# Held-back projection pieces, masks woven into two products, and rotating PSUM banks in a graph-attention kernel

## The reference, cut to what matters

```python
# x: 1250 x 768; src, dst: 41250 edges (20000 random ones in both directions, and loops)
def _L0_gnn_ref(x, edge_index, W, b):
    src, dst = edges plus one loop for each node
    deg = segment_sum(1, dst); dis = rsqrt(deg)
    return segment_sum((x @ W)[src] * (dis[src] * dis[dst]), dst) + b

def gat_conv(x, edge_index, W, a_src, a_dst, bias, heads, out_ch, concat):
    xl = (x @ W).reshape(n, heads, out_ch)
    e = leaky_relu((xl * a_src).sum(-1)[src] + (xl * a_dst).sum(-1)[dst], 0.2)
    e = exp(e - segment_max(e, dst)[dst])
    alpha = e / (segment_sum(e, dst)[dst] + 1e-16)
    out = segment_sum(xl[src] * alpha, dst)
    return (heads side by side, or their mean) + bias

def _L1_gnn_ref(x, ...):
    h1 = relu(layer_norm(gat_conv(x, W1, ..., heads 4, 256 each))) + (x @ Wr1 + br1)
    return layer_norm(gat_conv(h1, W2, ..., 1 head of 768)) + (h1 @ Wr2 + br2)

x = _layernorm(x + _L0_gnn_ref(x, edges, W0, b0))
x = _layernorm(x + _L1_gnn_ref(x, edges, ...))
```

## Time and profile before

| | |
|---|---|
| median of 3 runs | 905.65 us (905.5 to 906.43) |
| the profiled execution | 904.68 us, of it 902.9 us from its first instruction to its last (the span) |
| mean granted clock of PE | 0.968 of full speed |
| busy | PE 836.2 us, VectorE 679.6 us, ScalarE 256.1 us, GpSimd 60.4 us |
| counting, to the last degrees | about 21 to 156 us |
| first aggregation | 161 to 229 us |
| masks | 230 to 246 us |
| projection `xl`, residual product | 246 to 413 us |
| first attention | 415 to 621 us |
| second layer | 621 to 903 us |

### The profile page before, as it was taken

How to read it: one execution, slowest core, us unless ns; L and a number is a source line. 1 busy time by engine, 2 the same in 40 slices (tenths; PEclk the granted TensorE clock), 3 DMA queues, 4 the chain that set the end, 5 groups by cost and what they waited for, 6 DMA issues and landing times.

```text
span 902.9 us, 13798 instructions
## 1 busy us (share of the span) xinstructions
PE 836.2 (93%) x5086; PEld 546.4 (61%) x5086; DVE 679.6 (75%) x1180; ACT 256.1 (28%) x451; POOL 60.4 (7%) x82
## 2 busy tenths in 40 slices
PE   2999999899699999999999988968999999999995
PEld 2577776466555444446888867856656666655553
DVE  5988885778656668797777789783985579955686
ACT  3344443500012010114444354341213118730000
POOL 2000001000202000100000000000210000000021
PEclk8799999899899999999999989989999999999998
DMA  8000000314221213513210113210222732322231
GB/s 289 2 1 2 2 2 22 139 46 163 95 110 47 70 34 120 192 66 136 90 50 30 29 48 105 63 37 1 70 70 71 245 111 71 105 71 70 70 105 67
DMA packets 23373, 70.42 MB, mean 78 GB/s; under 512 B 2628, under 2 KB 3548, under 8 KB 23182
## 3 DMA queue, kind: packets, MB, share of 16 engines
q1 hardware_dynamic: 21438, 61.80, 19.6%
q0 software_dynamic: 1872, 7.78, 2.7%
HBM read 49.26 MB, written 20.31 MB: 77 GB/s over the span
## 4 chain that ended last, share of the span: by engine, by line
PE 72%; DVE 12%; issue 11%; POOL 2%; ACT 1%; DMA 1%; DVEq 0%; SPq 0%; POOLq 0%; ACTq 0%
PE psum L636 24%; PE psum L817 14%; PE psum L788 13%; PE psum L879 11%; PE psum L665 4%; DVE arena L1323 2%; DVE arena L1338 2%; DVE arena L1354 1%; DVE arena L1186 1%; PE psum L670 1%; DVE arena L1362 1%; POOL arena L570 1%; DVE arena L1228 1%; PE psum L661 1%; PE psum L838 1%
## 5 line engine op out<-in xcount | busy, mean ns | idle before, releaser
L636 PE MATMUL psum<-arena 128*128 128x512 f16 (+1 forms) x1080 | 228.9, 364 | 0.9 <-DVE arena L1213 0.9
L817 PE MATMUL psum<-arena 128*128 128x257 f32 x800 | 181.6, 389 | 22.2 <-ACT arena L953 20.9
L886 ACT ACTIVATE arena<-psum 128x160 uint16<-128x160 f32 (+6 forms) x226 | 94.9, 465 | 332.7 <-PE psum L636 79.5
L817 PEld LDWEIGHTS psum<-arena 128*128 128x128 f32 x800 | 154.7, 195 | 47.8 <-issue 16.6
L636 PEld LDWEIGHTS psum<-arena 128*128 128x128 f16 x1080 | 100.4, 98 | 104.1 <-issue 5.3
L788 PE MATMUL psum<-arena 128*128 128x512 f16 x960 | 159.2, 328 | 2.4 <-ACT arena L953 2.4
L788 PEld LDWEIGHTS psum<-arena 128*128 128x128 f16 x960 | 94.4, 98 | 65.0 <-ACT arena L953 2.8
L879 PE MATMUL psum<-arena 128*128 128x512 f16 (+2 forms) x600 | 98.4, 326 | 0.0
L961 ACT ACTIVATE arena<-arena 128x640 f32<-128x640 f32 x80 | 66.0, 829 | 87.4 <-DVE arena L1323 87.4
L1228 DVE CUSTOM_DVE_ANT_0 arena<-psum,arena 128x256 bf16<-128x256 f32 (+1 forms) x100 | 46.7, 527 | 52.5 <-PE psum L636 33.1
L1218 DVE CUSTOM_DVE_ANT_0 arena<-arena 128x1280 bf16<-128x1280 bf16 x50 | 71.0, 1487 | 16.7 <-DMA arena<-as_scratch 12.9
(11 more groups left out here) (162 smaller groups left out, 618.4 us busy)
## 6 DMA issues: line engine op xcount, KB each, us to landing
arena<-in_L_gnn_W_dram SPq DMA_DIRECT2D x14, 384.0 KB, 5.9
r_scratch<-arena SPq DMA_DIRECT2D x10, 512.0 KB, 2.6
arena<-uv_scratch SPq DMA_DIRECT2D x16, 320.0 KB, 3.9
arena<-r_scratch SPq DMA_DIRECT2D x10, 512.0 KB, 3.6
x_scratch<-arena SPq DMA_DIRECT2D x10, 384.0 KB, 4.6
arena<-x_scratch SPq DMA_DIRECT2D x10, 384.0 KB, 3.5
r_scratch<-arena SPq DMA_DIRECT2D x10, 384.0 KB, 2.6
arena<-r_scratch SPq DMA_DIRECT2D x10, 384.0 KB, 4.0
```

What stands on the lines that cost most here:

```text
L636: ins = pe.matmul(o[:, a:b], part[:, k, ds(t * P, P)], w[:, k, a:b], start=(not begun and k == 0 and n == 0 and m == 0), stop=(k == kn - 1 ...
L817: last = pe.matmul(p_att[:, j, 0:HID + 1], pf[n % PSLOTS][:, j * P:(j + 1) * P], xl[ch % H][:, k, 0:HID + 1], start=(k == 0), stop=(k == T ...
L886: act.activation(out_, in_, ACT.Copy, scale=scale).then_inc(signal, 1)
```

## The change

Three things, in one diff.

1. **Held pieces.** The last five pieces of the projection of tile 9 (`HELD`) are taken out of the counting loop and stand behind the last degrees, ahead of the flag's matmul. The other pieces are spread over the same 80 blocks, 49 where 54 were, so that a tile takes about nine blocks. The transposes of tile t + 2 stand in the block after the one in which tile t ends (`FETCH`: blocks 8, 17, 26, 35, 44, 53, 61 and 70), VectorE's part of them five blocks later, and ScalarE reads a finished tile in the block in which it ends. ScalarE reads tile 9 between the third and the fourth `hs_hi`.
2. **Masks woven in.** The first product starts behind the first two transposes, and the ten mask transposes, with the transposes of tiles 2 and 3, stand between the six parts of the first product and the six of the second. `x1t_low(0)` stands on VectorE ahead of the normalising of tile 9. The masks' slots move to banks 6, 7 and 0, 1. The copy of the first product stands behind the last mask on VectorE.
3. **Banks in rotation.** Chunk 0 uses banks 0 to 4, chunk 1 banks 5, 6, 7, 0, 1, and so on over eight banks; the second four chunks go over six banks. Each chunk's first matmul into a bank waits for that bank's last reader. `sums` takes one instruction for each run of neighbouring banks: two in chunks 1, 3, 4, 5 and 6.

```diff
+HELD = 5
+FETCH_LAG = 5
+HS_FIRST = 3
 def pieces_until(b):
-    return max(0, min(b + 1 - W_LAG, KD)) if b < SUBS else KD + (b + 1 - SUBS) * (T - 1) * KD // (NB - SUBS)
+    return max(0, min(b + 1 - W_LAG, KD)) if b < SUBS else KD + (b + 1 - SUBS) * ((T - 1) * KD - HELD) // (NB - SUBS)
+def done_block(t):
+    return next(b for b in range(NB) if pieces_until(b) >= (t + 1) * KD)
+FETCH = {done_block(t) + 1: t + 2 for t in range(T - 2)}
+ATT_BANKS = [[(ch * C1 + j) % 8 for j in range(C1)] for ch in range(H)]
+ATT_BANKS += [[(4 + ch * C1 + j) % 6 for j in range(C1)] for ch in range(H)]
...
-        X1_ORDER = [s for i in range(T) for s in [("tr", t) for t in (2 * i, 2 * i + 1) if t < T] + [("xl", i)]]
+        X1_ORDER = [("tr", 0), ("tr", 1)]
+        X1_ORDER += [s for k in range(KD) for s in [("part", 0, k)] + ([("neg", k - 3)] if k >= 3 else [])] + [("xl", 0)]
+        X1_ORDER += [s for k in range(KD) for s in [("part", 1, k)] + [[("neg", 3)], [("tr", 2)], [("neg", 4), ("tr", 3)], [("neg", 5), ("neg", 6)], [("neg", 7)], [("neg", 8), ("neg", 9)]][k]] + [("xl", 1)]
+        X1_ORDER += [s for i in range(2, T) for s in [("tr", t) for t in (2 * i, 2 * i + 1) if t < T] + [("xl", i)]]
...
 (PE, counting)
-                if j == 0 and 1 <= t < T - 1:
-                    transposes(t + 1)
+                if b in FETCH:
+                    transposes(FETCH[b])
...
             for t in range(T - TAIL, T):
                 degrees(t)
+            for q in range(T * KD - HELD, T * KD):
+                project_nodes(q // KD, q % KD)
             pe.wait_ge(S["over_ok"], 1)
...
 (PE, attention)
-                    if k == 0 and ch:
-                        pe.wait_ge(S["att_read"], (ch - 1) * C1 + j + 1)
+                    if k == 0 and bank_reader(ch, j):
+                        pe.wait_ge(S["att_read"], bank_reader(ch, j))
...
 (ScalarE)
             for t in range(T):
+                if t == HS_FIRST:
+                    node_evict(T - 1)
+                    act.wait_ge(S["h_read"], T)
                 act.activation(hs_hi[:, t, :], ...
...
 (VectorE)
                 dve.tensor_tensor(y, y, par_rows[:, 2, 0:D], ALU.add).then_inc(S["dve"], 1)
+                if t == T - 1:
+                    x1t_low(0)
...
-                dve.tensor_scalar(ssum, p_att[:, :, HID:HID + 1]..., SOFTMAX_EPS, None, ALU.add)
+                for a, b in bank_runs(ch):
+                    first = ATT_BANKS[ch][a]
+                    dve.tensor_scalar(ssum[:, a:b], p_att[:, first:first + b - a, HID:HID + 1]..., SOFTMAX_EPS, None, ALU.add)
```

135 lines of the change are left out of this document (80 added, 55 removed).

## The result

| | before | after |
|---|---|---|
| median | 905.88 us (4 runs, 905.5 to 906.43) | 894.88 us (4 runs, 893.02 to 895.81) |
| the profiled execution | 904.68 us, span 902.9 | 893.02 us, span 891.1 |
| mean granted clock of PE | 0.968 | 0.980 |

The changed kernel takes 0.9875 of the time (95% interval 0.9858 to 0.9893): 11.0 us won, where 8.1 were forecast. In a second set of runs, beside the experiments, it was 895.14 against 905.33, 0.9882 (0.9864 to 0.9901), 10.2 us. 897.5 was forecast, with a range from 892.5 to 901.0. The direction was right, and the size 2 to 3 us too small. One execution of one experiment, the transposes one block later, took 4842.58 us and is left out of its median and ratio.

The account below looks back on a forecast made before the run. The chain of waits was taken as the bound, PE holding most of it. Held pieces 0.5 + masks 3.8 + banks 3.8 = 8.1 us won, 905.65 − 8.1 = 897.5 us for the median; range 892.5 to 901.0.

Parts of the forecast that it names:

- All three terms: Counting loop and behind it: five pieces removed win 4.95 us; seven transpose waits cost 3.1, the late flag 1.3.
- The four small waits: Woven masks: PE waits 0.75 us ahead of mask transposes 4 and 5, then 0.35 and 0.6 at the end.
- the half fall of the clock: Woven masks: a clock fall behind PE's new wait would cost 1.85 us; half was counted, 0.9.
- The first number of the sum: Woven masks: PE waits 2.0 us for `x1t_low(0)` before the first product, in 2.0 + 24.7 + 2.45 = 29.2 us.
- The gain per start: Attention, starts of chunks 1 to 3: PE's wait for ScalarE's eviction goes, 1.08 us each, 3.24 in all.
- the second sum: Attention: a second `sums` instruction on VectorE where a chunk's banks are split, costing 0.19 us.
- VectorE is the bound there: Second four attention chunks: VectorE mostly bounds, so waits ahead of chunks 5 to 7 stay; 0.25 us won each time.
- the matmul done ahead: Attention chunks 5 to 7: one matmul of five goes early into a free bank, 0.44 less 0.19 us each time.
- Covered transposes: Rival, counting loop: transposes of x never wait, held pieces give 3.6 us, 11.2 in all, 894.4 us; chance 0.15.
- Rotation that doesn't free the chunks: Rival, attention: the wait returns at the fourth matmul, rotation gives 0.5 of 3.8 us, 900.8 us; chance 0.13.
- The woven stretch at 1.2 GHz: Rival, masks and first products: PE's clock stays low, 14.8 us lost there, 10.5 slower in all, 916 us; chance 0.03.

Follow-up runs that it names:

- the two experiments: Each against the changed kernel: transposes of x one block later, 892.37 us; the flag's matmul behind the first held piece instead of the fifth, 893.67 us.
- the early sums: Changed kernel with chunk 6's sums 3.6 us earlier on VectorE and its eviction one step earlier, 889.04 us; with chunks 4 and 5 earlier too, 888.19 us.
- the same group: Changed kernel run again beside the held pieces undone (0.9887), masks put back (0.9934) and banks fixed (0.9948); ratios to the kernel before; changed kernel 895.14 us, 0.9882.
- the rotated traces: Seven traces with banks in rotation: two of the changed kernel, five of variants; 115.46 to 118.23 us from the sums of chunk 3 to the first product behind the attention.
- the changed kernel's second trace: Trace of the changed kernel run once more, nothing altered; median 895.14 us, ratio 0.9882 to the kernel before; the trace's span 894.2 us.
- the last three with early sums: Changed kernel with sums of chunks 4 to 6 earlier, 888.19 us; plus later transposes and earlier flag, 882.82; plus two W2 row blocks a step later, 877.89.
- the second trace of before: Trace of the kernel before run once more, nothing altered; 906.59 us.

## Why the prediction was right, and where it was too small

*Held pieces (0.5 forecast, 0.3 shown).* All three terms stood. Seven new waits came at the seven places, at 0.43 us each against 0.44 (the kernel with the transposes a block later). The loop became shorter by 2.87 − 0.93 = 1.94 us in the first pair of traces, and by 1.74 against the kernel without held pieces; 1.85 was worked out. `hs_lo` came 1.34 to 1.41 us late behind the degrees (1.5 forecast), and the flag was the cause. That the part is worth almost nothing followed from the sum, and the two experiments show that 3.5 and 0.9 us more were to be had in it.

*Masks (3.8 forecast, 5.3 in the stretch).* The walk through the order was close: 24.7 us of work, and 3.94 us of waits against 2.0 + 2.45. The four small waits were 2.00 instead of 2.45. The term that was mis-sized is the half fall of the clock: behind 1.94 us PE stayed at 1.00 in all ten traces with this wait, so 0.9 us too much was given back. Some chance of it was there: behind the 2.44 us from which it was read the clock fell in ten of the fourteen traces, and ahead of the attention it fell once behind 2.25 us. Its price was off as well: where the fall does come, it costs 2.93 us, since it lies over the products and lasted 6.0 us, and not the 1.85 that the transposes had shown. The first number of the sum, the 2.0 us wait, decided the sign: with 5.61 us in its place the same weaving loses 1.4 us against none, in the traces.

*Banks (3.8 forecast, 5.0 to 5.5 shown).* The mechanism was right: matmuls into free banks go ahead, and the waits at the starts of chunks 1 to 3 vanish. Two terms were mis-sized. The gain per start is 1.31 and not 1.08: 50 matmuls take 21.68 us from start to start, and the row's 21.91 includes a tail that overlaps what follows, so the idle time printed behind it was 0.23 too short. I divided that 21.91 by 50 as well, with little harm. And the second sum costs 0.07 (0.23 against 0.16), not 0.19, because the two overlap. In the second four chunks 1.1 to 1.6 us were won instead of 0.56. The statement behind that term, that VectorE is the bound there, failed in chunk 7: PE's wait ahead of it lies on the path, as the early sums showed, so the matmul done ahead counted there in full, 24.36 to 23.87 us from PE's start to the last sums. The 0.5 us of chunk 5 are as much, which says the same of the stretch behind its wait.

*The sum.* 0.9 for the fall, 0.45 for the small waits, 0.7 for the starts of chunks and 0.5 to 1.0 for the second four, less 0.2 for the held pieces, make 2.4 to 2.9: 8.1 and these are 10.5 to 11.0, against 10.2 to 11.0 measured. The parts account for the whole: undone one at a time they cost 0.0005, 0.0052 and 0.0066 of the time, together 0.0123, and the change won 0.0118 in the same group.

*The rivals.* Covered transposes: eight rows of 0.39 us say no. Rotation that doesn't free the chunks: no wait at three starts. The woven stretch at 1.2 GHz: the clock was 1.00 in all of it, through four small waits and turns from bank to bank; by the Trainium skill, TensorE: Matmul & The Clock Gate, A second HAM failure mode, it would have gone up and down, and the trace doesn't show that. Even behind 5.61 us it came back after 6.0, well before the third product.

*The range.* It was made for the sum's terms and held. It had no term for the clock behind the waits of the attention, which by the line through the rotated traces moves an execution by up to 2.5 us (0.48 for each of 14.1 − 8.8), more than any error of the sum.

## What to carry to other kernels

Where PE waits for another engine's result, look first at what stands ahead of that result on its engine: one instruction moved in front of a normalisation was worth 5.8 us here by the ratios (0.9946 − 0.9882) and 6.6 in the traces, and without it the reordering around it lost 1.4. A wait on PE's path costs its own length and, where the clock falls, up to 3 us more behind it, so its removal can be worth more than the row says. And an idle row behind pipelined matmuls is shorter than the time that can be won: take the period between two like events instead.

## What the runs showed of the hardware

- Behind the same wait of 4.1 us, at the same place, PE ran at 1.2 GHz for 2.9 to 6.1 us (rotated banks), by execution; this and the start of the first block make up 2.4 of the 3.0 us between the two traces of the changed kernel.
- PE's clock did not fall behind waits of 1.07 (start of chunk 5 with the early sums) and 1.94 us, and fell behind all of 3.12 us and more in the changed kernel's attention. Behind 3.45 us it fell in two kernels and stayed in one (the sums of chunk 6 alone earlier).
- Waits between these are a matter of the execution. The wait of 2.44 us ahead of the first product behind the attention is the same in all fourteen traces; the clock fell behind it in ten and stayed in four (the changed kernel's second trace and the last three with early sums). Ahead of the attention PE waited 1.64 to 2.37 us in the twelve traces of changed kernels; the clock fell in one of them, behind 2.25 us, and chunk 0 reached its sums 23.63 us behind its start instead of 21.95. In the second trace of before it fell 1.9 us behind the end of a wait of 1.50.
- Two sum instructions over different banks joined to 0.22 to 0.23 us, where one took 0.16 to 0.17.
- The float32 matmul of 257 columns, two records in the trace, takes 21.68 / 50 = 0.434 us at full clock.
